# A four-layer gated cross-attention and expert stack on one Trainium2 core: a later state update, four more output buffers, and an opening of the last attention with its sums in another order

## The reference, cut to what matters

```python
x = x + tanh(g_xattn[0]) * L0_xattn(layernorm(x), ctx, ctx, mask)  # 16 heads of 16
x = x + tanh(g_ffn[0])   * L0_ffn(layernorm(x))                    # 16 experts, 4 per row, gated (silu)
x = x + tanh(g_xattn[1]) * L1_xattn(layernorm(x), ctx, ctx)        # one head of 256
x = x + tanh(g_ffn[1])   * L1_ffn(layernorm(x))                    # 2 local attention layers + GLU
x = x + tanh(g_xattn[2]) * L2_xattn(layernorm(x), ctx)             # 16 heads
x = x + tanh(g_ffn[2])   * L2_ffn(layernorm(x))                    # 16 experts, 4 per row, + a shared one
x = x + tanh(g_xattn[3]) * L3_xattn(layernorm(x), ctx, ctx)        # 16 heads, phase rotation
x = x + tanh(g_ffn[3])   * L3_ffn(layernorm(x))                    # a linear filter by FFT, + bias
```

```python
att = softmax(Q @ K.T / 16);  X = layer_norm(Q + att @ V)          # gamma, beta
return layer_norm(relu(X @ W1 + b1) @ W2 + b2 + X)                 # gamma, beta
```

## Time and profile before

| | us |
|---|---|
| runs of the kernel before | 1762.08, 1763.86, 1765.33 (median 1763.86) |
| profiled execution: its own time | 1762.41 |
| its span | 1760.6 |
| TensorE busy | 1662.8 (94%) |
| VectorE busy | 1132.2 (64%) |
| ScalarE busy | 984.9 (56%) |
| GpSimd busy | 940.0 (53%) |
| `L0f_tiles`, 79 tiles | about 211 to 361 |
| `L1x`, 16 sequences | about 361 to 484 |
| `L3x`, 16 sequences | about 1563 to 1758 |

### The profile page before, as it was taken

One profiled execution on the slowest core, in us unless ns is written; L12 is line 12 of the kernel. 1 busy time (PEld: TensorE's weight loads), 2 busy tenths in 40 slices (PEclk: granted clock), 3 DMA queues, 4 the chain that ended last, 5 costly groups with the idle time before them and its releaser, 6 DMA issues. The chain is left out here.

```text
span 1760.6 us, 38383 instructions
## 1 busy us (share of the span) xinstructions
PE 1662.8 (94%) x11883; PEld 1301.1 (74%) x11928; DVE 1132.2 (64%) x3349; ACT 984.9 (56%) x2789; POOL 940.0 (53%) x1138
## 2 busy tenths in 40 slices
PE   7999799989789999999999999989998999989998
PEld 4777478858646777777777777768876888867886
DVE  4787666638656666766667676547886353337875
ACT  4677445524435566665666656547772355536775
POOL 2366675535446655665555655333677244447752
PEclk9999899999999999999999999999999999999999
DMA  4333276565020000000000000012445344432200
GB/s 155 96 103 117 98 234 196 165 209 180 21 107 4 6 4 4 4 5 5 4 4 4 5 5 4 5 49 79 148 145 183 94 128 146 134 133 77 76 26 25
DMA packets 79670, 140.28 MB, mean 80 GB/s; under 512 B 11729, under 2 KB 61105, under 8 KB 77297
## 3 DMA queue, kind: packets, MB, share of 16 engines
q1 hardware_dynamic: 65744, 98.22, 17.9%
q0 software_dynamic: 13728, 39.60, 6.4%
HBM read 84.88 MB, written 50.82 MB: 77 GB/s over the span
## 5 line engine op out<-in xcount | busy, mean ns | idle before, releaser
L1545 POOL TENSOR_TENSOR L1f_rn<-L1f_ss,L1f_root_c 128x8 f32<-128x8 f32 x64 | 105.9, 1655 | 183.1 <-DVE L1f_ss L1848 181.4
L1681 PE MATMUL L1f_psQ<-L1f_xT,arena 128*128 128x128 f32 x1408 | 172.4, 275 | 0.9 <-ACT L1f_xT L1756 0.9
L1681 PEld LDWEIGHTS L1f_psQ<-L1f_xT,arena 128*128 128x128 f32 x1408 | 169.5, 192 | 4.4 <-ACT L1f_xT L1756 1.1
L1774 ACT ACTIVATE L1f_sg<-L1f_psQ,vec1f 128x128 f32<-128x128 f32 x192 | 63.5, 364 | 137.2 <-PE L1f_psQ L1681 137.1
L2073 POOL DMA_INDIRECT outs_L2f<-L2f_tiles_ys,L2f_tiles_spot x79 | 76.0, 962 | 119.1 <-ACT L2f_tiles_ys L2218 110.0
L1560 POOL TENSOR_TENSOR L1f_rot<-L1f_qn,L1f_sinT 128x512 f32<-128x512 f32 x64 | 113.4, 1792 | 28.8 <-DVE L1f_qn L1864 28.8
L1894 DVE SCALAR_TENSOR_TENSOR L1f_hid<-L1f_psQ,vec1f,L1f_sg 128x128 f32<-128x128 f32 x192 | 61.4, 346 | 92.1 <-ACT L1f_sg L1774 91.9
L1605 PE MATMUL L1f_psQ<-arena,L1f_hT 128*128 128x512 f32 x256 | 118.4, 605 | 0.6 <-ACT L1f_hT L1763 0.6
L2073 POOL DMA_INDIRECT outs_L0f<-L0f_tiles_ys,L0f_tiles_spot x79 | 76.0, 962 | 48.0 <-ACT L0f_tiles_ys L2218 42.7
L1693 PE MATMUL L1f_psB<-arena,L1f_hid 128*128 128x256 f32 (+1 forms) x384 | 99.8, 388 | 0.0
L1550 POOL TENSOR_TENSOR L1f_pr<-L1f_pr,L1f_rs 128x512 f32<-128x512 f32 x64 | 95.6, 1515 | 6.2 <-DVE L1f_rs L1858 6.2
(11 more groups left out here) (533 smaller groups left out, 4642.6 us busy)
## 6 DMA issues: line engine op xcount, KB each, us to landing
L0f_tiles_xs<-rows_L0f SPq DMA_DIRECT2D x79, 144.0 KB, 2.4
L2f_tiles_xs<-rows_L2f SPq DMA_DIRECT2D x79, 144.0 KB, 2.3
arena<-in_w_L2f SPq DMA_DIRECT2D x8, 1120.0 KB, 6.2
arena<-in_w_L1f SPq DMA_DIRECT2D x8, 1088.0 KB, 7.5
L1x_got<-outs_L0f SPq DMA_DIRECT2D x16, 512.0 KB, 4.0
L3x_got<-outs_L2f SPq DMA_DIRECT2D x16, 512.0 KB, 3.4
arena<-in_w_L0f SPq DMA_DIRECT2D x8, 768.0 KB, 4.9
rows_L0f<-zero SPq DMA_DIRECT2D x31, 144.0 KB, 2.7
```

What stands on the lines that cost most here:

```text
L1545: nc.gpsimd.tensor_tensor(rn[:, s.p, h], ss[:, s.p, h], root_c[:, 0:LH], ALU.pow).then_inc(s_rn, 1)
L1681: mm = nc.tensor.matmul(out, w, xT[:, k], start=(k == 0), stop=(k == KC - 1), skip_group_check=True)
L1774: nc.scalar.activation(sg[to, u], unit_out(u, 0, of), ACT.Gelu, bias=column(s, 2 * KC + u)[of]).then_inc(s_sg, 1)
```

## The change

Three places, independent of each other.

In `L1x`, `(update, -4)` moves in VectorE's list from the third place to the one behind `tops`. No instruction is added.

In `L0f_tiles`, `ys`, `pair`, `spot` and the semaphores of the scatters get 12 buffers in place of 8. The second expert phase keeps 8.

In `L3x`, on GpSimd the roots of sequences 0 and 1 stand ahead of the sum in their round, the others stay behind it; on VectorE the statistics of sequences 2 and 3 move to the end of their round, behind `queries`; the two biases are multiplied by their gates on VectorE, ahead of its first round, and GpSimd only waits for that.

```diff
-YR = 8
+        self.outputs = 12 if ready else 8
-        self.s_out = [sem(f"out{i}") for i in range(YR)]
+        self.s_out = [sem(f"out{i}") for i in range(self.outputs)]
+def summed_by_vector(fn):
+    return lambda s: fn(s) if s.n < SWIFT else None
+def summed_by_gpsimd(fn):
+    return lambda s: fn(s) if s.n >= SWIFT else None
+def opening_sums(fn):
+    return lambda s: fn(s) if SWIFT <= s.n < 2 * SWIFT else None
+def other_sums(fn):
+    return lambda s: None if SWIFT <= s.n < 2 * SWIFT else fn(s)
# GpSimd, heads_attention
             def bias_row(s):
-                if s.n == 0:
+                if s.n == 0 and store is not None:
+                    pool.wait_ge(s_bias, 1)
+                    pool.wait_ge(s_gbf, 1)
+                elif s.n == 0:
...
-                    if store is not None:
-                        c.dma_wait(pool, "L3b", 1)
-                        nc.gpsimd.tensor_scalar(gbf[:, :], gbf[:, :], c.gates[:, gate_f:gate_f + 1], None, ALU.mult).then_inc(s_gbf, 1)
-                        pool.wait_ge(s_gbf, 1)
-            each_round([(gather, 5), (roots, 3)] * (gathered is not None) + [(row_roots, 4)] * (gathered is None)
+            each_round([(summed_by_vector(roots), 3), (gather, 5), (summed_by_gpsimd(roots), 3)] * (gathered is not None) + [(row_roots, 4)] * (gathered is None)
# VectorE, heads_attention
+            if store is not None:
+                dve.wait_ge(s_bo, 1)
+                nc.vector.tensor_tensor(gbo[:, :], psB[:, 0:D], bo, ALU.add).then_inc(s_b, 2)
+                dve.wait_ge(s_b, 4)
+                nc.vector.tensor_scalar(gbo[:, :], gbo[:, :], c.gates[:, gate:gate + 1], None, ALU.mult).then_inc(s_bias, 1)
+                c.dma_wait(dve, "L3b", 1)
+                nc.vector.tensor_scalar(gbf[:, :], gbf[:, :], c.gates[:, gate_f:gate_f + 1], None, ALU.mult).then_inc(s_gbf, 1)
             def bias_row(s):
...
-                dve.wait_ge(s_bo, 1)
-                nc.vector.tensor_tensor(gbo[:, :], psB[:, 0:D], bo, ALU.add).then_inc(s_b, 2)
+                if store is None:
+                    dve.wait_ge(s_bo, 1)
+                    nc.vector.tensor_tensor(gbo[:, :], psB[:, 0:D], bo, ALU.add).then_inc(s_b, 2)
-            each_round([(gather, 4)] * (gathered is not None) + [(row_stats, 4)] * (gathered is None)
+            each_round([(other_sums(gather), 4)] * (gathered is not None) + [(row_stats, 4)] * (gathered is None)
                        + [(at(turned, 2), 0), (queries, 2)]
+                       + [(opening_sums(gather), 4)] * (gathered is not None)
# VectorE, single_attention
-            each_round([(centre, -2), (rows, 1), (update, -4), (add, 2), (attended, -1), (tops, 0), (last_stats, -3)], LOW, HIGH + 1)
+            each_round([(centre, -2), (rows, 1), (add, 2), (attended, -1), (tops, 0), (update, -4), (last_stats, -3)], LOW, HIGH + 1)
# expert_tiles
-    XR, W, G = 6, 2 * P, NB // 2
+    XR, YR, W, G = 6, r.outputs, 2 * P, NB // 2
```

## The result

| | before | after |
|---|---|---|
| runs, median (lowest to highest) | 1765.33 (1762.08 to 1766.29, five) | 1749.94 (1747.88 to 1754.27, five) |
| profiled execution, its span | 1762.41, 1760.6 | 1750.75, 1748.9 |

The ratio is 0.9915, with a 95% interval from 0.9897 to 0.9932: 15.0 less (12.0 to 18.2), where 14.1 had been worked out.

The account below looks back on a forecast made before the run. TensorE was taken as busiest but not gapless: a TensorE-VectorE loop, a stop at tile 16 and a late opening bound three phases. Savings 5.8 + 6.0 + 2.3 = 14.1 gave 1748.3 to 1749.8, said as 1749.0; range 1745.5 to 1756.

Parts of the forecast that it names:

- Part 1: Single attention: `update` moved behind the maxima leaves the TensorE-VectorE loop, rounds 6.08 to 5.46; 5.8 saved, ends 1.5 and 6.5.
- The 0.4 taken off for the first round: Single attention: 6.2 worked out for ten rounds, taken as 5.8, a little off for the first round.
- My remark that `add` has room: Single attention: `add` waits at most 0.3 for the combined rows, which VectorE's round of 5.25 has room for.
- Part 2: Expert phase: twelve buffers end three scatter waits and the half clock behind tile 16; 6.0 saved, ends 0 and 7.1.
- Part 3: Last attention's opening: normed rows right behind sequence 1's statistics, 2.5 earlier, 0.2 lost; 2.3 saved, ends 2.5 and 0.
- the root: Last attention: sequence 0's root stood behind GpSimd's first sum, ended at 1576.94, and VectorE normed at 1577.04.
- the moved statistics: Last attention: statistics of sequences 2 and 3 come later, two pairs now ahead of the first maxima; 0.2 lost.
- The sum: Whole kernel: 5.8 + 6.0 + 2.3 = 14.1 saved, since phases do not overlap; 1749.0 said.
- Port lock: Rival, 11%: single attention, GpSimd's root blocks the moved `update` for its 0.57; 3.2 less gain, 1752.2.
- SP: Rival, 11%: expert phase, late fetches make TensorE wait at tiles 19 to 22, lower clock returns; 1754.0.
- Half clock elsewhere: Rival, 5%: half-clock stretches of 3.0 each caught in other phases; slower by over 0.2% from six, 1767.
- The text put one at 3.0: Cost of one half-clock stretch, read at tile 16 in the expert phase as 6.28 - 3.24 = 3.0.

Follow-up runs that it names:

- e2: Only the twelve buffers in the expert phase, on the kernel before; 1760.44, ratio 0.9970.
- e4: The changed kernel with `update` just ahead of the maxima, between `attended` and `tops`; 1758.22, ratio 0.9964 to the kernel before.
- e10: The kernel before, eight buffers, with 12 filler products in TensorE's stop ahead of tile 16's turn; 1764.41 against 1763.12, once each.
- e3: Only the last attention's edits, on the kernel before; 1761.30, ratio 0.9980.
- e7: The kernel before with only GpSimd's roots of sequences 0 and 1 ahead of its sum; normed rows 2.44 behind the statistics, against 2.58; no total given.
- e12: The changed kernel once more, on a fourth chip where the kernel before takes 1800.01; 1795.37, ratio 0.9961.

## Why the prediction was right

**Part 1, 5.8.** Measured 6.46 in the ten rounds, near the upper end. The round came out at 5.42 for 5.46, VectorE's list at 5.29 for 5.25 (420.25 to the end of the statistics at 425.54), `update` at 0.48 as said. The 0.4 taken off for the first round was not needed. The phase as a whole is 8.2 shorter, since it also lost a stretch at half clock; e2 and the changed kernel, both without one, differ by 6.3. My remark that `add` has room was right by only 0.18; the loop through the combined rows, which makes that figure, was not in the text, and e4 shows that it binds at once when anything is put between `add` and the maxima.

**Part 2, 6.0.** The turn of tile 16 came at 243.25 for 243.3. The mis-sized term is what comes after: tile 19 at 248.69 for 248.2. A tile behind a stop takes 2.09 and not 1.62 (243.25 to 245.34), with 0.17 of idle ahead of its hidden product; that start-up I had not counted. Small stops of 0.1 to 0.3 at the hidden products of tiles 18 to 30 take another 0.5; the profile puts them to issue, and their cause is open. At the last tile's turn 4.85 of the gain is left, at the phase's end 4.5, since from that turn on it takes 10.3 where it took 10.0. That 0.3 comes with the twelve buffers (perhaps the four more waits at the phase's end; no run tests it): 10.3 in all six profiles with twelve, 10.0 to 10.1 in all eight with eight, nine or ten. By e10 2.6 of the 4.5 is the clock.

**Part 3, 2.3.** e3: 2.3 at full clock, 13.4 to 14.0 for 15.66 to the first maxima. The exact figure is in part luck: the two waits give 1.6 to 2.3, and 0.6 of e3's came ahead of them. The text named one wait, the root; it put the moved statistics down as a cost only, where e7 shows that they were a second wait that had to go as well. From the phase's start the first maxima are 2.1 earlier (26.8 to 24.7). In the profile of the changed kernel the clock took 1.7 back.

**The sum.** 6.5 + 4.5 + 2.3 = 13.3, where I had 14.1, and 15.0 [12.0 to 18.2] was measured; the interval holds both, so that the median came within 1 of 1749.0 is in part luck. The profiled pair is 11.7 apart, because the half clock fell elsewhere: out of the single attention (1.7 gained), into `L1f` and `L3x` (3.4 lost).

**Rivals.** Port lock: `update`, from 424.60 to 425.07, lies beside GpSimd's root from 424.88 and isn't slowed, but it started first. One in the changed kernel starts when a root has begun, as the rival has it, and keeps its 0.48:

```profile
435.73 0.56 POOL L1259 TENSOR_TENSOR L1x_r<-L1x_v,half 128x1 f32<-128x1 f32 x1
```

```profile
435.79 0.48 DVE L1456 SCALAR_TENSOR_TENSOR X<-L1x_t,L1x_rg,X 128x256 f32<-128x256 f32 x1
```

SP: the steps behind tile 16 are 2.09 at most, and none brought the lower clock. Half clock elsewhere: it was taken up, but given back as well. The stretches add up to 27.3 before and 22.4 after. The text put one at 3.0; that one was 6.8 long, and one of 3.4 moved a phase by about 1.7 (`L1f`, 675.0 to 676.7). In `L0x` 6.8 of half clock before, against 3.5 after, cost nothing that shows: 201.8 in both. That the gain hangs on the chip was no case of mine: the 6.0 rested on when VectorE came to tile 13 against the landing of tile 5's scatter, and where the first tiles come later no gain shows.

## What to carry to other kernels

Write the loops through two engines down as sums, and all of them, also those with a product that is made early in the next round: a piece belongs behind the last instruction that another engine waits for. Before buffers are added, look for the wait's second price, the half clock behind TensorE's stop; in e10 fillers in the stop bought that part alone. When an edit removes one of two waits that end together, judge it only with the other, and read a phase's gain from a profile in which its clock is full.

## What the runs showed of the hardware

**Half clock behind short stops.** Stretches of 3.4 at 0.50 followed stops of TensorE of 1.75 (last attention) and of 1.95 and 2.12 (local attention), and one of 6.8 followed the stop of 2.76 at tile 16; 3.4 cost some 1.7, the 6.8 about 3. Not each such stop brings one: in e12 the last attention had none, with the same code, and the longer stop of 3.07 had none behind it. With filler products in the stop the clock was full at all three places, in one profile each: at tile 16, where the other three profiles with eight buffers on such a chip (stops of 1.90 to 3.40) had it at half; in the local attention's second opening round, where ten of the thirteen other profiles had; and in the last attention, where e12 and e3 were full without them. So only tile 16 speaks for the fillers, and one profile is thin.

**VectorE beside GpSimd.** Two kinds of instruction were slowed by GpSimd's 256-wide additions in SBUF: `update`, with two SBUF inputs (0.88 for 0.48), and the normalisation, with one (up to 0.95 for 0.40). The later they start in GpSimd's addition the less they lose. Most `update` instructions of the kernel before start 0.13 into it and end 1.01 after its start; this one starts 0.48 into it, is hardly slowed, and ends 1.01 after its start too:

```profile
444.84 0.73 POOL L1235 TENSOR_TENSOR X<-X,L1x_gb 128x256 f32<-128x256 f32 x1
```

```profile
445.32 0.53 DVE L1428 SCALAR_TENSOR_TENSOR X<-L1x_t,L1x_rg,X 128x256 f32<-128x256 f32 x1 [0.64 <-issue]
```

The normalisations of the last attention (L361) do the same: eleven in the kernel before start 0.02 to 0.28 into such an addition, take 0.86 down to 0.60, and all end 0.87 to 0.88 after its start; one that starts 0.49 into it takes its 0.40. So VectorE's instruction ends as if it stood still until about 0.5 after GpSimd's started, and then ran at full speed. The Trainium skill, "SBUF — State Buffer", section "SBUF: two separate sides", says that the loser fully blocks; that fits, but the block ends some 0.2 before GpSimd's recorded end (GpSimd's spans are rough in the profile). The addition from PSUM (`add` at 422.09, 0.42, beside L1263 at 422.22) started first, and neither was slowed. Beside the one-column root `update` was not slowed, started before it or after it (435.79), and a root that started under `update` took 0.61 in place of 0.57.

**The same kernel on other chips.** 1765, 1763, 1800 and 1805 for the kernel before. In e7 the phases `L0x`, `L0f_tiles`, `L2x` and `L2f_tiles` are 9.6, 12.5, 12.3 and 9.6 longer than in the kernel before on the first chip, and the others differ by at most 2.0, about one stretch at half clock; ScalarE stops in the second of them without a releaser in the profile.
